# A fused post-norm decoder layer: whole projections between longer stretches of cross-attention, and stacks issued block by block

## The reference

```python
x = layernorm(x + self_attention(x))   # 16 heads of 32, LoRA of rank 16 on q, k, v, o
x = layernorm(x + cross_attention(x, ctx))
x = layernorm(x + ffn(x))              # fp8 e4m3 rounding, gelu gate, 512 -> 2048 -> 512

def cross_attention(x, c):             # 16 heads of 16; the 256 rows are the channels
    q = Wq @ x + bq; k = Wk @ c + bk; v = Wv @ c + bv      # (B, 256, 512)
    scores = einsum('bhkt,bhks->bhts', q, k) / 4           # per head 512 x 512
    out = einsum('bhts,bhks->bhkt', softmax(scores), v)
    return Wo @ out + bo
```

## Time and profile before

| | us |
|---|---|
| runs | 2080.48, 2097.97, 4479.71; median 2097.97 |
| the profiled execution | 2092.57, of it the span 2090.7 |
| PE busy | 1969.1 (94% of the span), clock 0.953 of full on average |
| DVE, ACT, POOL busy | 1506.7, 1131.6, 979.2 |

### The profile page before, as it was taken

The page is one execution under the profiler, slowest core; times in us unless marked ns, Lnnn a source line. Parts: engine busy times, 40 slices in busy tenths (PEclk is TensorE's granted clock), DMA queues, the critical chain, the costliest instruction groups (busy, mean ns, idle before and its releaser), DMA issues.

```text
span 2090.7 us, 31790 instructions
## 1 busy us (share of the span) xinstructions
PE 1969.1 (94%) x11460; PEld 1054.3 (50%) x11460; DVE 1506.7 (72%) x2632; ACT 1131.6 (54%) x2117; POOL 979.2 (47%) x968
## 2 busy tenths in 40 slices
PE   7798999999999888999999999999999898999998
PEld 4576776767677643344444434433444333444443
DVE  3455666675656656788878878777888728999997
ACT  3233444444444424687878877777788673333331
POOL 3345555555455422244444434444344226666664
PEclk9899999999999868899999999999999889999999
DMA  5877787878777733465665565655565610111111
GB/s 151 136 140 137 144 154 124 171 126 146 138 132 141 144 56 64 96 105 128 122 124 106 105 112 108 108 100 106 98 113 93 166 40 11 51 41 41 41 61 41
DMA packets 149515, 220.56 MB, mean 105 GB/s; under 512 B 41463, under 2 KB 50167, under 8 KB 148615
## 3 DMA queue, kind: packets, MB, share of 16 engines
q1 hardware_dynamic: 139694, 216.95, 53.2%
q10 hardware_dynamic: 9664, 1.58, 0.6%
HBM read 83.95 MB, written 32.02 MB: 55 GB/s over the span
## 4 chain that ended last, share of the span: by engine, by line
PE 53%; DMA 20%; DVE 11%; POOL 6%; ACT 3%; issue 3%; SPq 3%; ACTq 0%; POOLq 0%; DVEq 0%
PE bank L1302 8%; PE bank L1596 8%; PE bank L1267 7%; PE bank L85 6%; DMA xa_sums<-xa_oc 5%; DMA sa_kst<-sa_part_kl 5%; PE bank L1572 4%; PE bank L86 4%; PE bank L87 4%; DMA inv<-xa_sums 4%; PE bank L1310 4%; PE bank L567 3%; DMA xa_den<-inv 3%; PE bank L622 2%; DVE xa_mneg L1345 2%
## 5 line engine op out<-in xcount | busy, mean ns | idle before, releaser
L1345 DVE TENSOR_REDUCE xa_mneg<-bank 128x1 f32<-128x512 f32 x1024 | 657.9, 681 | 200.8 <-PE bank L1310 197.4
L1167 ACT ACTIVATE xa_prob<-bank 128x512 f32<-128x512 f32 x1024 | 568.8, 600 | 211.7 <-PE bank L1302 202.5
L1310 PE MATMUL bank<-xa_kst,xa_qst 48*128 48x512 f32 x1024 | 414.6, 477 | 19.1 <-DVE xa_mneg L1345 14.5
L1302 PE MATMUL bank<-xa_qst,xa_kst 49*128 49x512 f32 x1024 | 400.9, 463 | 16.1 <-ACT xa_prob L1167 15.9
L458 ACT ACTIVATE sa_prob<-bank 128x512 f32<-128x512 f32 x256 | 152.4, 598 | 370.7 <-PE bank L622 370.1
L1302 PEld LDWEIGHTS bank<-xa_qst,xa_kst 49*128 49x128 f32 x1024 | 162.8, 190 | 333.1 <-ACT xa_prob L1167 259.0
L1267 PE MATMUL bank<-xa_prob,xa_v 128*32 128x512 f32 x2048 | 285.5, 631 | 0.0
L1504 POOL TENSOR_TENSOR ff_total<-ff_prod,ff_mag 128x512 f32<-128x512 bf16 x128 | 194.5, 1520 | 108.9 <-DVE ff_mag L1620 108.9
L692 DVE TENSOR_REDUCE sa_mneg<-bank 128x2 f32<-128x512 f32 x256 | 164.2, 682 | 51.6 <-PE bank L635 51.3
L1310 PEld LDWEIGHTS bank<-xa_kst,xa_qst 48*128 48x128 f32 x1024 | 165.1, 191 | 55.1 <-DVE xa_mneg L1345 39.0
L1548 ACT ACTIVATE ff_gelu<-bank 128x512 bf16<-128x512 f32 x128 | 75.5, 592 | 161.2 <-PE bank L1596 161.1
(11 more groups left out here) (191 smaller groups left out, 3729.9 us busy)
## 6 DMA issues: line engine op xcount, KB each, us to landing
xa_qst<-xa_part_q SPq DMA_DIRECT2D x192, 128.0 KB, 5.3
xa_kst<-xa_part_k SPq DMA_DIRECT2D x192, 128.0 KB, 6.4
sa_qst<-sa_part_qh SPq DMA_DIRECT2D x64, 256.0 KB, 6.3
sa_kst<-sa_part_kh SPq DMA_DIRECT2D x64, 256.0 KB, 8.8
xa_den<-inv SPq DMA_DIRECT2D x64, 256.0 KB
sa_xraw<-xT SPq DMA_DIRECT2D x8, 1024.0 KB, 8.2
sa_qst<-sa_part_ql SPq DMA_DIRECT2D x32, 256.0 KB, 6.0
sa_kst<-sa_part_kl SPq DMA_DIRECT2D x32, 256.0 KB, 10.2
```

The source lines that it names most:

```text
L1167: act.activation(prob[:, e % XPROBS, :], banks[eb[e]][:, :], ACT.Exp, scale=X_SCALE)\
L1302: pe.matmul(banks[eb[e]][:, :], kst[u % 3][rows_of, head // 2, t * P:(t + 1) * P], qst[u % 3][rows_of, head // 2, :], start=True, stop=Tru ...
L1310: pe.matmul(banks[mb[m]][:, :], qst[u % 3][rows_of, n // 8, t * P:(t + 1) * P], kst[u % 3][rows_of, n // 8, :], start=True, stop=True).the ...
L1345: dve.tensor_reduce(mneg[:, u % 2, column:column + 1], banks[mb[m]][:, :], AX.X, ALU.max, negate=True).then_inc(s_mfree, 1)
```

## The change

- **Cross-attention.** `project_part` is called for both halves in one slot: q at 2, k at 10, o at 18, v at 26. `values` is called at the slots EXP_AT + 9 and EXP_AT + 12 of every eight, that is in slots 5 and 8 (mod 8), not each fourth slot. A unit's 32 slots are so cut into stretches of 2, 3 and 3 slots, twelve in all, where there were sixteen of 2. The copy out of `pj` comes 3 slots after the projection, for k 6 slots (`LEAVES`). EXP_AT is two slots later, OUT_AT three; the later steps of the output come closer after it (den at +13 and not +14, the multiplication at +17 and not +21, the sum at +34 and not +39, `oh` at +35 and not +41). The ring of `prob` grows from 12 to 16 tiles. The loads of c and x, and their splits, move to other slots.
- **Stacks.** Each DMA of a stack has its own slot in SP's stream (cross: q 20 to 25, k 26 to 31; self: q S, S, S + 1, k S + 1, S + 2, S + 2).
- **Start and self-attention inputs.** Wq is loaded ahead of xT; xT comes in four DMAs, one for each 128 rows, each with its own semaphore; LoRA factors of v and q are cut before x; the banks of the merged weights are chosen anew.
- **FFN.** The seventh of its early slots goes from 1108 in place of 1106, and four of its tiles lie elsewhere.

```diff
-    STACK_AT = {"q": S, "k": S + 1}
+    STACK_AT = {"q": (S, S, S + 1), "k": (S + 1, S + 2, S + 2)}
...
-    merge_bank = {"v": (3, 4, 5, 6), "q": (0, 1, 2, 7), "k": (3, 4, 5, 6), "o": (3, 4, 5, 6)}
+    merge_bank = {"v": (3, 4, 5, 6), "q": (1, 2, 7, 3), "k": (4, 5, 6, 7), "o": (3, 4, 5, 6)}
...
         load_w("v")
-        load_xraw(sp, wait, 0)
-        for n in "qko":
-            load_w(n)
+        load_w("q")
+        for c in range(DC):
+            load_xraw(sp, wait, 0, c)
+        load_w("k")
+        load_w("o")
...
-            for r, m in enumerate(parts):
-                sp.dma_start(dst[u % 3][r * SDH:(r + 1) * SDH].bitcast(F32),
-                             part[name + m][:, :].bitcast(F32)).then_inc(s_st[u % 3], 16)
+            sp.dma_start(dst[u % 3][r * SDH:(r + 1) * SDH].bitcast(F32),
+                         part[name + parts[r]][:, :].bitcast(F32)).then_inc(s_st[u % 3], 16)
...
+        wait.wait_ge(s_lora, 16 * 6)
+        high_lora("v")
+        high_lora("q")
         for c in range(DC):
             high_x(act, wait, 0, c)
-        wait.wait_ge(s_lora, 16 * 6)
-        for n in "vqk":
-            high_lora(n)
+        high_lora("k")
...
-XPROBS = 12
+XPROBS = 12, 16
...
-    MAX_AT, TURN_AT, EXP_AT = S + 8, 2 * S + 10, 2 * S + 18
+    MAX_AT, TURN_AT, EXP_AT = S + 8, 2 * S + 10, 2 * S + 20
     BATCH = 2 * S
-    OUT_AT = EXP_AT + 19
+    GROUP = 4
+    VALUES_AT = (EXP_AT + 9, EXP_AT + 12)
+    OUT_AT = EXP_AT + 22
...
+    LEAVES = {"q": 3, "k": 6, "v": 3, "o": 3}
+    slot_of = {}
     for u in range(U):
-        part_slots["q", u] = [S * u + 2, S * u + 6]
-        part_slots["k", u] = [S * u + 10, S * u + 14]
+        slot_of["q", u] = S * u + 2
+        slot_of["k", u] = S * u + 10
     for b in range(NB):
-        part_slots["v", b, 0] = [BATCH * b + 26, BATCH * b + 30]
-        part_slots["v", b, 1] = [BATCH * b + 50, BATCH * b + 54]
-        part_slots["o", b, 0] = [BATCH * (b + 2) + 58, BATCH * (b + 2) + 62]
-        part_slots["o", b, 1] = [BATCH * (b + 3) + 18, BATCH * (b + 3) + 22]
+        for t in range(CC):
+            slot_of["v", b, t] = BATCH * b + S * t + 26
+            slot_of["o", b, t] = BATCH * (b + 2) + S * t + 50
...
-            if (un := output_half(slot, 14)):
+            if (un := output_half(slot, 13)):
                 u, half = un
                 wait.wait_ge(s_back, 16 * (2 * u + half + 1))
...
-            if (un := unit(slot, STACK_AT, 1)):
-                stack("q", un[0])
-            if (un := unit(slot, STACK_AT + 5, 1)):
-                stack("k", un[0])
-            if (b := batch(slot, -40)):
+            for n, name in enumerate("qk"):
+                if (un := unit(slot, STACK_AT + 6 * n, 6)):
+                    stack(name, *un)
+            if (b := batch(slot, -28)):
                 load_c(sp, wait, b)
-            if (b := batch(slot, -27)):
+            if (b := batch(slot, -24)):
                 load_x(sp, wait, b)
...
-            if (un := output_half(slot, 21)):
+            if (un := output_half(slot, 17)):
...
-            if (un := unit(slot, OUT_AT + 39, 1)):
+            if (un := unit(slot, OUT_AT + 34, 1)):
...
-            if (un := unit(slot, OUT_AT + 41, 1)):
+            if (un := unit(slot, OUT_AT + 35, 1)):
...
-            if (b := batch(slot, -18)):
+            if (b := batch(slot, -14)):
                 high_x(act, wait, b)
...
-            if (un := unit(slot, EXP_AT + 34, 1)):
-                values(un[0], 7)
-            if (un := unit(slot, EXP_AT + 6, S - 7)) and un[1] % 4 == 0:
-                values(un[0], un[1] // 4)
+            for odd in range(2):
+                if (un := unit(slot, VALUES_AT[odd])) and un[1] % (2 * GROUP) == 0:
+                    values(un[0], un[1] // GROUP + odd)
...
-            for job, i in parts_in.get(slot, []):
-                project_part(job, i)
+            for job in jobs_in.get(slot, []):
+                for i in range(2):
+                    project_part(job, i)
...
-FFN_AT = [1022, 1046, 1070, 1078, 1086, 1094, 1106]
+FFN_AT = [1022, 1046, 1070, 1078, 1086, 1094, 1108]
```

More of the change, by code:

```diff
@@ L325, in sync @@
             for name in "qk":
-                if (un := unit(slot, STACK_AT[name], 1)):
-                    stack(name, un[0])
+                for r, at_slot in enumerate(STACK_AT[name]):
+                    if (un := unit(slot, at_slot, 1)):
+                        stack(name, un[0], r)
             i = round_tile(slot, 0)
@@ L349, in sync @@
                       .then_inc(s_xnat[n % 4], 16)
-            p, left = divmod(slot - 4, S * SG)
-            if left == 0 and p + 1 < PAIRS:
-                load_xraw(sp, wait, p + 1)
+            p, c = divmod(slot - 4, S * SG)
+            if 0 <= c < DC and p + 1 < PAIRS:
+                load_xraw(sp, wait, p + 1, c)
     def gpsimd(pool):
@@ L831, in cross_attention_phase @@
     of = parts.sb("xa_of", [P, D], F32)
-    ol = mem("output").sb("xa_ol", [P, 2, groups, D], F32R)
+    output = mem("output")
+    ol = output.sb("xa_ol", [P, 2, groups, D], F32R)
+    prob += [output.sb(f"xa_prob{n}", [P, D], F32) for n in range(*XPROBS)]
     r = mem("cross_small")
@@ L878, in cross_attention_phase, with in_turn @@
     m_at = {job: n for n, (_, _, job) in enumerate(sorted(m_order, key=lambda m: m[:2]))}
[L881 to L883 removed]
+    def in_turn(count, few, more, begin):
+        places = [few[n % len(few)] if n < begin else more[n % len(more)] for n in range(count)]
+        before = [max((m for m in range(max(0, n - 2 * len(more)), n) if places[m] == places[n]), default=None)
                   for n in range(count)]
[L885 removed]
+        return places, before
     mb, mb_before = in_turn(len(m_order), (3, 4), (3, 4, 1), (S + 1) * 4)
     eb, eb_before = in_turn(S * U, (5, 6), (5, 6, 0), S * 2)
+    place, prob_before = in_turn(
+        S * U, range(XPROBS[0]), [*range(*XPROBS), *range(XPROBS[0])], S * 2)
     SLOTS = range(max(slot_of.values()) + 12)
@@ L1015, in sync @@
                     one_rows(sp, n)
-            if (un := unit(slot, TURN_AT + 1, 1)):
+            if (un := unit(slot, TURN_AT + 2, 1)):
                 u = un[0]
@@ L1080, in gpsimd @@
             yield
-            for job in ends_in.get(slot - 2, []):
-                if job[0] in "qk":
-                    name, u = job
+            for name in "qk":
+                for job in jobs_in.get(slot - LEAVES[name] - 1, []):
+                    if job[0] != name:
+                        continue
+                    u = job[1]
                     n = 2 * u + "qk".index(name)
@@ L1110, in gpsimd @@
                     .then_inc(s_ol, 1)
-            if (b := batch(slot, -17)):
+            if (b := batch(slot, -13)):
                 low_x(pool, wait, b)
-            if (b := batch(slot, -8)):
+            if (b := batch(slot, 1)):
                 low_c(pool, wait, b)
-            for job in ends_in.get(slot - 3, []):
+            for job in jobs_in.get(slot - 5, []):
                 if job[0] == "o":
@@ L1164, in scalar @@
                 wait.wait_ge(s_e, e + 1)
-                wait.wait_ge(s_av, (e - XPROBS) // 4 + 1)
-                left.values(wait)
-                act.activation(prob[:, e % XPROBS, :], banks[eb[e]][:, :], ACT.Exp, scale=X_SCALE)\
+                if prob_before[e] is not None:
+                    wait.wait_ge(s_av, prob_before[e] // GROUP + 1)
+                elif place[e] < XPROBS[0]:
+                    left.values(wait)
+                else:
+                    left.output(wait)
+                act.activation(prob[place[e]][:, :], banks[eb[e]][:, :], ACT.Exp, scale=X_SCALE)\
                    .then_inc(s_exp, 1)
@@ L1170, in scalar @@
                 u, half = un
-                wait.wait_ge(s_av, S // 4 * u + 4 * half + 4)
+                wait.wait_ge(s_av, S // GROUP * u + 4 * half + 4)
                 if half == 0:
@@ L1177, in scalar @@
                 act.activation(oc[half][:, :], ob[:, :], ACT.Copy).then_inc(s_oc[half], 1)
-            for job in ends_in.get(slot - 1, []):
+            for job in [job for name in "qkv" for job in jobs_in.get(slot - LEAVES[name], []) if job[0] == name]:
                 n = at[job]
@@ L1188, in scalar @@
                     _, b, t = job
[L1189 removed]
+                    wait.wait_ge(s_av, S // GROUP * 2 * (b - 1))
                     if b % 2:
@@ L1206, in scalar @@
                 act.activation(oh[:, u // 2 % 2, u % 2], of[:, :], ACT.Copy).then_inc(s_oh, 1)
-            for job in ends_in.get(slot - 6, []):
+            for job in jobs_in.get(slot - 6, []):
                 if job[0] == "o":
@@ L1358, in vector @@
                 dve.tensor_copy(mrow[:, u % 2, :], banks[mb[m]][0:32, 0:P]).then_inc(s_mfree, 1)
-            for job in ends_in.get(slot - 1, []):
+            for job in jobs_in.get(slot - LEAVES["o"], []):
                 if job[0] == "o":
```

108 lines of the change are left out of this document (50 added, 58 removed).

## The result

The changed kernel takes 2235.9 us (median of 4 runs, 2226.29 to 2246.39) against 2092.44 for the kernel before on the same chip: ratio 1.0713, 95% interval 1.0662 to 1.0763. It is 7% slower; 2072 us was forecast. The profiled span is 2232.9 us against 2090.7. Of these 142 us, cross-attention holds most: from its first maximum to its last it takes 1806.8 - 756.5 = 1050.3 us in place of 1679.1 - 737.4 = 941.7, so 108.6 more. Self-attention's last maximum comes 19.1 us later (745.3, was 726.2), and 14.5 us are added behind cross-attention.

What follows compares the result with a forecast made beforehand. PE was taken to bound the kernel, losing time to changes of matmul kind and waits. Savings of 40.3 and 11.5 us against 22.4 given back, with smaller terms, made -19.9 on 2092.57: 2072 us, range 2036 to 2104.

Steps and rivals of the forecast that it cites:

- Part 1, fewer changes of kind: Cross-attention: fewer switches between kinds of matmul save PE 1.44 us a unit, 40.3 us over 28 units.
- Part 2, k then o: Cross-attention, ahead of o's projection: PE waits 0.8 us a unit for the late copy of k, 22.4 us lost.
- the walk: Slot-by-slot timing of the new cross-attention order from row durations; it had ACT end the copy of k at 5.14 us.
- Part 2, the DVE behind o: Cross-attention maxima behind o's output tile: PE's loss grows from 1.10 to 1.24 us, 0.14 a unit, 3.9 us.
- the sum: Whole kernel: all terms add to -19.9 us, giving 2072 us; a unit goes from 27.35 to 26.6 us.
- Part 2, `oh`: Cross-attention's output sum: PE's wait of 0.82 us, once a batch, goes; 11.5 us taken back.
- Part 3, self-attention's stacks: Self-attention: the last two k blocks, moved one slot later, cost 4 us, ends 0 and 16.
- Part 4, the start: Kernel start: Wq, loaded second, arrives by 15 us; gain 0 to 6.5 us, taken as 4.
- Part 5, the ends: Change-over to cross-attention costs 4 us, ends 0 and 8; two more slots before the exponentials cost 1.6 us.
- Rival C: Cross-attention: waits at o's and v's projections make the clock fall, about 5 us each; 2128 to 2198 us; chance 0.06.

Runs made afterwards that it cites:

- without the chain: Changed kernel with the sums' transfer, reciprocal, inversion and denominators left out from the second unit on, all stack blocks sent: 2072.7 us, ratio 0.9926.
- the first run: Changed kernel with all six cross-attention k stack blocks sent at slot 26, ahead of the sums' transfer: 2279.81 us, ratio 1.0966.
- the two runs without the chain: Changed kernel and kernel before, each with the sums, reciprocal, inversion and denominators left out from the second unit on: 2072.7 and 2050.68 us.
- half of the blocks: Changed kernel and kernel before, each without six of a unit's twelve stack blocks from the fourth unit on: 2109.15 and 2056.33 us.
- the last run: Changed cross-attention, self-attention as before, stacks at once, chain moved later, plus `oh` at 41, `ol` at 43, second read back at 16, v at 27: 2158.54 us.
- the last run but one: Changed cross-attention, self-attention as before, stacks issued at once, second half's chain four slots later, first half's denominators at 21: 2205.67 us, ratio 1.0547.

## Why the prediction was wrong, step by step

- **Part 1, fewer changes of kind: right.** A merged projection lasts 1119.48 - 1117.92 = 1.56 us (forecast 1.61), three slots 1114.01 - 1113.11 = 0.90 (0.91), the values 1.00 still.

```profile
1113.11 0.49 PE L1319 MATMUL bank<-xa_qst,xa_kst 49*128 49x512 f32 x1
...
1114.01 1.07 PE L1284 MATMUL bank<-xa_prob,xa_v 128*32 128x512 f32 x8
1115.01 0.50 PE L1319 MATMUL bank<-xa_qst,xa_kst 49*128 49x512 f32 x1
...
1117.92 0.47 PE L85 MATMUL bank<-xa_oh,xa_woh 128*128 128x512 f32 x1
...
1119.48 0.50 PE L1319 MATMUL bank<-xa_qst,xa_kst 49*128 49x512 f32 x1
```

- **Part 2, k then o: mis-sized.** 22.4 us forecast, 3.1 us on PE measured. ACT runs ahead of the walk.
- **Part 2, the DVE behind o: its growth mis-sized the other way.** I took the 1.10 us of the earlier trace rows as paid in each unit before, and so charged only 0.14 more. After, the stretch of two slots lasts 1125.20 - 1123.41 = 1.79 us for 0.67, so PE loses 1.12 (forecast 1.24), though the trace's own wait there is only 0.27:

```profile
1123.41 0.49 PE L1319 MATMUL bank<-xa_qst,xa_kst 49*128 49x512 f32 x1
...
1125.20 0.38 PE L85 MATMUL bank<-xa_wvh,xa_ch 128*128 128x256 f32 x1
```

  It is so in 22 of 23 units at full clock in 850 to 1640. Before, a loss of 0.9 us or more behind o stands in 3 of 27. The growth is about 1 us a unit, not 0.14. This and the term above nearly cancel, which is why the unit without the chain comes out near the forecast. The terms of the sum, by the way, give 25.5 / 28 = 0.91 us a unit, not the 0.75 between 27.35 and 26.6.
- **Part 2, `oh`: there was little to take back, and the reasoning failed.** ACT's wait at `oh` was 6.6 us in 9 units before and is 4.7 in 4 after; PE's for the exponentials went from 8.7 to 7.1. That is far from the 11.5 us of the sum. I saw the second half's store and read leave the stacks' slots (now 3 and 7) and put the sums at "inversion due at 6.6 us (8 slots)", as though due were done. The change moved the sums' own transfer from slot 22, between q and k, to slot 27, into the row of k's blocks. The earlier trace rows had its price: 6.84 us with two rows of stacks about it. In the unit shown it is 1134.61 - 1127.41 = 7.2 us, and behind all twelve blocks, in the first run, 10 us.
- **The missing term.** The sum has no line for cross-attention's twelve stack DMAs, although the change moves eleven of them, k's by one to six slots and q's by up to five, and the sums in among them. This is the step that failed: an overlap was put at nothing without a reason. The trace of before had it. SP's timeline there:

```profile
1008.20 3.84 SPq L989 DMA_DIRECT2D xa_qst<-xa_part_q  x6
1012.45 0.60 SPq L1029 DMA_DIRECT2D xa_sums<-xa_oc  x1
1013.09 3.77 SPq L989 DMA_DIRECT2D xa_kst<-xa_part_k  x6
```

  Issue ends at 1016.86, and a block of k lands 6.4 us behind its issue by the page's median: 15.1 us from slot 20. By the landing times of all units it is 16.1 (median, up to 18.6), and the first use comes at 18.8, in some units right behind the landing; `s_e` forbids an earlier start. A window that is some 85% full has little room for a wait for ACT between its blocks. Measured: 48.7 / 21 = 2.3 us a wait on PE, nearly once a unit, and a fall of the clock with it.
- **Part 3, self-attention's stacks: direction right, size low.** 4 us forecast, 12 measured for the whole changed phase, inside its ends of 0 and 16.
- **Part 4, the start: right in sign.** PE waited 4.48 us for Wq in place of 6.55 and began it at 16.75 (forecast: by 15); the first maximum comes 1.9 us earlier, not 4.
- **Part 5, the ends: low.** 5.6 us forecast; from cross-attention's last maximum to the end it takes 14.5 us more (426.1 for 411.6), still 6.6 more without the chain (417.4 for 410.8). No run takes this apart.
- **Rival C had the mechanism of the cost, not its place.** "If each did, 25 x 5 = 125, 2198": 24 falls in 24.7 units, 2236. I put the trigger at the projections of o and v; it was the blocks. Its argument against, that a like wait in each unit had left the clock at 1.00, misread before, where the loss of 1.1 us behind o is rare. The run without the chain bears it out all the same: there the stretch behind o loses 1.1 us in each unit and the clock is 1.00 from 900 to 1500. What drew the falls were longer waits: in after, a fall began during each of the 15 single waits of over 2 us, or within 2 us of its end. The Trainium skill's page TensorE: Matmul & The Clock Gate (A second HAM failure mode) tells of micro-idles between groups as banks are cycled; this trace shows falls behind single long waits for a transfer instead.
- **The sum.** The 143.5 us split by the two runs without the chain: after is 163 us above its own, before 42 above its own, so 121 us hang on the chain, its transfers and the waits for them, and 22 remain between the two without it (self-attention's 12 among them).

**Shown:** the chain of sums and the stacks in one window cost most of the time. Without the chain the distance between the two kernels falls from 143 us to 22, with half of the blocks to 53. Order on the queue, another queue and earlier starts do not bring it back. **Open:** whether a full placement exists in which nothing waits; the last run won back some 65 of the 163 us between after and the run with no chain, both counted with the self-attention of before (an estimate from its 12 us). A run that keeps the chain but sends `den` without its 256 KB was not made, so the share of mere bytes in the 121 us is not separated.

## What to carry to other kernels

When a change shifts one chain's phase, list every transfer of both chains by slot, with its bytes, its landing time and the slot of its first use, and look at windows that are already nearly full; a term without a line in the sum is not zero. An engine that works in order turns a late small transfer into a late everything: the DVE's inversion of 128x16 elements took 0.25 us and held up maxima for 5. Judge a wait by what the clock does after it, too: here that doubled its price (2.3 us a wait for the blocks, and 55 / 24 = 2.3 us lost in a fall).

## What the runs showed of the hardware

- The sums' transfer of 8 KB, issued behind twelve blocks of 128 KB, was in use after some 10 us (first run); the store of the inverted sums, 8 KB too, took 2 us with nothing ahead. Issued from ACT's queue the sums were no faster (10.7 us, median of the units in which the DVE waited).
- The clock, by PE's single waits in 850 to 1640 that began at full clock. Over 2 us: 15 in after, 21 and 19 in the runs with k at slot 26 and with the sums on ACT's queue, 24 and 12 in the last two; a fall began during every one of these 91 or within 2 us of its end. Shorter: 24 of 1.2 us, one a unit, in the last run but one, and 23 of 0.7 to 1.2 us in the last; behind none of them did a fall begin within 3 us. After has 24 falls in all, mostly to between 0.5 and 0.8 over 5 us, and the kernel before 4.
